# Six of sixteen pieces of the last stage's first half beside the second convolution, and a third early band of x

## The chip, the cores and the metric

One core of one Trainium2 chip runs the whole program. The metric is device time in microseconds (us). All data is float32. PE is TensorE, DVE is VectorE, ACT is ScalarE, POOL is GpSimd and SP is SyncE; an engine with a q (SPq, ACTq) is the queue of DMA issues on it.

## The reference

x has 16 samples of 128 channels and 160 x 160 pixels. For each sample:

```
x_proj = einsum('bchw,oc->bohw', x, proj_w)                # 128 -> 64 channels
att1 = route(x_proj, ..., depthwise 3x3 or 5x5)            # the kernel size is chosen by an argmax
att2 = route(att1, ..., depthwise 7x7, 9x9 or 11x11, dilation 3)
out = concatenate([att1, att2], axis=1)
maps = concatenate([out.mean(1), out.max(1)])
gate = sum over the 2 outputs of sigmoid(conv7x7(maps) + sp_b)
return out * gate + x
```

route() takes the mean over all pixels, multiplies by a small matrix and picks the convolution with the largest logit. The last stage therefore has two halves: channels 0 to 63 are att1 * gate + x (the first half, "f1"), channels 64 to 127 are att2 * gate + x (the second half, "f2").

## The kernel before

The work is a software pipeline over the samples, written as turns s = 0 to 17. In turn s the sample s is projected and gets its first convolution (att1), the sample k = s-1 gets its second convolution (att2), the sample m = s-2 gets its maps, its gate and the second half of the last stage, and the sample n = s-3 gets the first half. Turns 4 to 14 are a loop, the others are written out. Turn 16 has no new sample, turn 17 ends the last two.

PE's order in a turn sets the order of the rest. First the projection (L858, with transposes L867): x is loaded by POOL in six bands of 32 rows (load_x, L533) into two buffers, RE and RO. Bands 0 and 1 are loaded in the turn before, beside the second convolution; each later band waits until the band two before it is summed and projected. After six of thirty fills PE transposes the maps of att2 (turn_map2, L870; MAPS_AFTER = 5). ACT copies the results into X (L710). Then comes the choice (route, L898) and the 7x7 convolution (L932).

Then the first convolution (conv1, L914): 16 groups of two channel pairs, the weights prepared by ACT (L734, L740) and the result copied back to X by ACT (L745). Behind each group PE does what the table AFTER (L62) names: "gt" spreads the gate, ("f2", u) is one of five parts of the second half (nine steps of three transposes, L953, each added to x by DVE, L1274), ("f1", u) is one of sixteen pieces of the first half. A piece has 10 rows of pixels. Its life: att1 is loaded from nat_d (load_at, two buffers, 400 KB), x is loaded (load_xa, three buffers, two DMAs of 200 KB), DVE multiplies by the gate (gate1, L1288), PE transposes ten times (finish1, L963), DVE adds to x (finish1, L1298), and the sum is stored from the same buffer (store_xa). POOL issues all of that (begin1, piece1). The second half's x, 720 KB a DMA, is loaded and stored by SP, two buffers (load_xf, store_xf), and between these SP "lands" the strips of the next second convolution in L (L439).

Then the second convolution (conv2, L967): 16 groups over L, the weights loaded by ACT's queue (L761), four pairs ahead, and doubled by POOL (L591); ACT gathers the input (bring, L765) and writes the result back (L775). Beside it DVE reduces X over the channels (reduce1, L1176 and L1177), sums bands 0 and 1 of the next x (take_x, L1101), and, when 24 of 32 pairs are evacuated, reduces L to mean and maximum maps (reduce2, L1198). SP stores att1 from X to nat_d in 24 DMAs of 256-byte runs (store_att1, L449), loads the gate in G1 (L468), and copies nat_d into overlapping strips (make_strips, L463, 18 DMAs).

X holds att1 from the first convolution until store_att1 and reduce1 are through; then it is unused until the next turn's ACT writes it. Tiles of pieces lie in RA and RX, for the last three samples (late, L317) in X.

A wait in these programs stands in the stream of its engine: what follows it on that engine waits too. PE's second fill of a projection waits until all sums of the last stage so far (f1_add, f2_add) are done.

## Time and profile before

| | |
|---|---|
| median of 3 runs | 6338.1 us (6338.06 to 6348.23) |
| the profiled execution | 6353.46 us, span 6351.9 us |
| PE, DVE, ACT, POOL busy | 77%, 49%, 45%, 20% of the span |
| DMA queue q1 (SP's), q0 (POOL's), q10 (ACT's) | 39.1%, 28.2%, 8.3% of 16 engines' span |
| moved | 1285.33 MB in 1015814 packets, mean 202 GB/s |
| a steady turn, from projection to projection | 372.2 us (2802.86 to 3175.06 us) |

The profile lists the busy time of each engine; an engine's idle time costs only where the chain that ends last passes through it. "DMA share" is the mean busy share of the 16 DMA engines. In rows of the timeline the bracket at the end is the idle time of that engine just before, with what ended it. All times below are of the one profiled execution.

### The profile page before, as it was taken

The numbers are of one execution on the slowest core, as the hardware profiler recorded it, in microseconds if no ns is written. First come the engines' busy times: TensorE is split into PE (matmuls) and PEld (weight loads), VectorE is DVE, ScalarE is ACT, GpSimd is POOL, SyncE is SP. The second block draws the span as 40 slices with busy tenths as digits, with TensorE's granted clock in tenths as the row PEclk, the third lists the DMA queues.
The fourth block names the chain that finished last, engine by engine and source line by source line (L and its number), as shares of the span: only waits on it lengthen the run. The fifth ranks groups of instructions, "written<-read, shape, count | busy, mean of one in ns | idle before, by whom it ended". The sixth has DMA issues, their size and how long they took to land.

```text
span 6351.9 us, 164601 instructions
## 1 busy us (share of the span) xinstructions
PE 4896.8 (77%) x62816; PEld 3336.1 (53%) x62816; DVE 3135.5 (49%) x3835; ACT 2832.8 (45%) x5378; POOL 1256.7 (20%) x2010
## 2 busy tenths in 40 slices
PE   5678897887878788787878888787887878885453
PEld 2236464655646465564745556464555646464342
DVE  3215445464545545464554545546544554645344
ACT  3455464544545455444544545354454535452120
POOL 2001011212112121211212121121212212121332
PEclk9889898898989889798988889898798979887675
DMA  9656758869697785968779696886969688696857
GB/s 225 182 133 188 174 160 217 228 182 237 191 229 198 215 223 179 227 212 217 210 194 231 180 230 207 214 227 172 233 181 242 199 217 234 179 224 156 226 131 189
DMA packets 1015814, 1285.33 MB, mean 202 GB/s; under 512 B 670750, under 2 KB 865737, under 8 KB 984414
## 3 DMA queue, kind: packets, MB, share of 16 engines
q1 hardware_dynamic: 855500, 578.24, 39.1%
q0 software_dynamic: 90800, 555.20, 28.2%
q10 hardware_dynamic: 69026, 146.11, 8.3%
q8 instruction: 218, 3.57, 0.2%
q14 instruction: 270, 2.20, 0.1%
HBM read 950.16 MB, written 456.70 MB: 221 GB/s over the span
## 4 chain that ended last, share of the span: by engine, by line
PE 36%; DMA 33%; DVE 11%; issue 10%; ACT 3%; POOL 2%; SPq 2%; ACTq 1%; POOLq 0%; DVEq 0%
DMA out_dram<-RX 15%; PE psC L984 13%; DMA RX<-in_x_dram 8%; DVE MM L1198 7%; DMA RX<-w_d 5%; PE psA L922 5%; PE psA L923 5%; PE psA L858 5%; PE psB L953 3%; PE psB L867 2%; DMA RX<-nat_d 2%; PE psB L932 2%; PE psB L963 2%; DVE RX L1274 1%; DVE L L1255 1%
## 5 line engine op out<-in xcount | busy, mean ns | idle before, releaser
L984 PE MATMUL psC<-RX 61*60 61x96 f32 (+7 forms) x49152 | 1457.6, 266 | 231.6 <-POOL RX L591 96.2
L984 PEld LDWEIGHTS psC<-RX 61*60 61x60 f32 x49152 | 1391.2, 132 | 304.3 <-issue 300.1
L1198 DVE TENSOR_REDUCE MM<-L 124x135 f32<-124x6480 f32 (+3 forms) x128 | 527.6, 4194 | 587.4 <-ACT L L775 587.4
L775 ACT ACTIVATE L<-psC 124x120 f32 (+4 forms) x2048 | 393.8, 284 | 830.0 <-PE psC L984 791.2
L858 PE MATMUL psA<-RX,projt 128*64 128x512 f32 x1920 | 577.0, 686 | 236.2 <-DMA RX<-in_x_dram 162.2
L922 PE MATMUL psA<-X,RX 128*128 128x240 f32 x1280 | 642.1, 591 | 125.4 <-ACT RX L740 125.3
L953 PE MATMUL psB<-ident,L 124*128 124x124 f32 x2160 | 445.5, 356 | 347.5 <-DVE RX L1274 286.6
L591 POOL COPY RX<-RX 64x720 f32<-64x720 f32 x512 | 402.3, 792 | 1455.4 <-DMA RX<-w_d 1454.4
L745 ACT ACTIVATE X<-psA,bias 128x246 f32<-128x246 f32 x1024 | 638.4, 737 | 62.6 <-PE psA L923 46.2
L923 PE MATMUL psA<-X,RX 128*128 128x240 f32 x1280 | 632.5, 583 | 0.0
L734 ACT ACTIVATE RX<-RX 32x640 f32<-32x640 f32 x320 | 233.8, 735 | 880.7 <-PE psA L923 749.9
L1274 DVE TENSOR_TENSOR RX<-psB,RX 128x360 f32<-128x360 f32 (+7 forms) x1200 | 370.2, 352 | 516.5 <-DMA RX<-in_x_dram 331.1
L765 ACT ACTIVATE RX<-L 128x1080 f32 (+1 forms) x256 | 541.7, 2124 | 136.3 <-DMA L<-strip_d 136.3
L953 PEld LDWEIGHTS psB<-ident,L 124*128 124x128 f32 x2160 | 313.5, 183 | 500.1 <-issue 476.8
L1288 DVE TENSOR_TENSOR RX<-RX,G 80x1280 f32<-80x1280 f32 x208 | 307.3, 1482 | 524.7 <-DMA RX<-nat_d 506.8
L704 ACT ACTIVATE RX<-psA 128x512 f32<-128x512 f32 x480 | 287.4, 599 | 558.1 <-PE psA L858 514.4
L867 PEld LDWEIGHTS psB<-ident,RX 128*128 128x128 f32 x1920 | 215.0, 148 | 481.6 <-ACT RX L704 333.4
L1176 DVE TENSOR_REDUCE MM<-X 128x246 f32<-128x15744 f32 x16 | 264.8, 16553 | 406.8 <-ACT X L745 406.8
L922 PEld LDWEIGHTS psA<-X,RX 128*128 128x128 f32 x1280 | 292.6, 241 | 307.2 <-issue 268.8
L1101 DVE TENSOR_REDUCE part<-RX 128x1 f32<-128x4480 f32 x96 | 442.0, 4604 | 0.0
L609 POOL DMA_DIRECT2D RX<-in_x_dram x416 | 220.2, 530 | 1078.1 <-DMA out_dram<-RX 1049.6
L923 PEld LDWEIGHTS psA<-X,RX 128*128 128x128 f32 x1280 | 301.0, 235 | 210.8 <-issue 173.6
(117 smaller groups left out, 5150.9 us busy)
## 6 DMA issues: line engine op xcount, KB each, us to landing
RX<-in_x_dram POOLq DMA_DIRECT2D x64, 2560.0 KB, 11.4
RX<-w_d ACTq DMA_DIRECT2D x512, 180.0 KB, 4.4
RX<-in_x_dram SPq DMA_DIRECT2D x128, 720.0 KB, 10.6
out_dram<-RX SPq DMA_DIRECT2D x128, 720.0 KB, 14.4
nat_d<-X SPq DMA_DIRECT2D x320, 280.0 KB
RX<-nat_d POOLq DMA_DIRECT2D x208, 400.0 KB, 6.8
RX<-in_x_dram POOLq DMA_DIRECT2D x416, 200.0 KB, 5.8
out_dram<-RX POOLq DMA_DIRECT2D x416, 200.0 KB, 4.9
```

The costliest lines, as they stand in the source:

```text
L591: nc.gpsimd.tensor_copy(w2t[j][64:128, :, :], w2t[j][0:64, :, :]).then_inc(w2_doubled, 1)
L745: ins = nc.scalar.activation(X[:, :, :, c:c + 1].rearrange("p b t c -> p (b t c)"), psA[pair % 2][:, ch * N1:(ch + 1) * N1], ACT.Identity, ...
L765: nc.scalar.activation(binf[q].rearrange("p (c f n) -> p c f n", c=G, f=5), Lc[:, :, bass.ds(g * G, G)].rearrange("p (n f) c -> p c f n", ...
L775: ins = nc.scalar.activation(dst[:, 0:NU2 - par, 15 * r:15 * r + nq, par, :], src[:, par:BR:2, :, :], ACT.Identity)
L858: ins = nc.tensor.matmul(o, projt[:, :], xsb[b % 2][:, :, w0:w0 + FW], start=True, stop=True)
L922: nc.tensor.matmul(o[:, :, 0:T1], w[:, ch, 96:224], rhs, start=True, stop=False, skip_group_check=True)
L923: ins = nc.tensor.matmul(o[:, :, 1:1 + T1], w[:, ch, 224:352], rhs, start=False, stop=True, skip_group_check=True)
L953: ins = nc.tensor.transpose(psB[t % 2][:, 124 * f:124 * f + 124], L[0:124, slot * C2:slot * C2 + 128], ident[0:124, 0:124])
L984: ins = nc.tensor.matmul(o[:, :, 0:kk, a:b], w2t[2 * q + p][rows, ch, z:z + PB], src[rows, 2 * p + ch, 0:nf, 3 * cg + dc:3 * cg + dc + kk, ...
L1101: nc.vector.tensor_reduce(part[:, b, 0:1], xs[:, own, :], AX.XY, ALU.add).then_inc(x_summed, 1)
L1198: nc.vector.tensor_reduce(dst[0:124, mm, :].rearrange("p (f b k) -> p f b k", f=9, k=3)[:, :, par:BR:2, :], src[:, :, 0:NU2 - par, :, par, ...
L1274: return nc.vector.tensor_tensor(d, view(psB[t % 2][rows, :], 64 * g0 + c0, sdims), d, ALU.add)
```

## The change

The pieces 0 to 5 of the first half (EARLY = 6) of sample m are taken from the next turn's first convolution and done in this turn, beside the second convolution. SP, and not POOL, loads and stores them, from buffers in the free X (bands 1 to 3 of it). On PE the first stands behind the twelfth of sixteen groups, the next four one behind each of the last four groups, the sixth right after the fifth. The table AFTER has only the pieces 6 to 15. The third band of x gets its own buffer in X (bands 4 and 5 of it) and is loaded by SP ahead of the strips. MAPS_AFTER goes from 5 to 8. reduce2 is cut in three (32, 16 and 16 channels), its first part beginning when half the pairs are evacuated. Samples 14 and 15 keep all pieces where they were.

```diff
-MAPS_AFTER = 5
+MAPS_AFTER = 8
+EARLY = 6
+AFTER = {0: (("f1", 6),), 1: (("gt", 0), ("f1", 7)), 2: (("f2", 0),), 3: (("f2", 1), ("f1", 8)),
+         4: (("f2", 2),), 5: (("f2", 3), ("f1", 9)), 6: (("f2", 4),), 7: (("f1", 10),), 8: (("f1", 11),),
+         9: (("f1", 12),), 10: (("f1", 13),), 11: (("f1", 14),), 12: (("f1", 15),), 13: (), 14: (), 15: ()}
...
+        xbuf = [t.rearrange("p (i w) -> p i w", w=W) for t in (RE, RO, Xf[:, 10496:15616])]
+        XBUF, XNTH, XPER = (0, 1, 2, 0, 1, 0), (1, 1, 1, 2, 2, 3), (3, 2, 1)
+                self.early = self.two and self.new
...
         def _(sp):
+            sp.dma_start(xbuf[2][:, :, :], x[0, :, 2 * ROUT1 - 2:2 * ROUT1 + 30, :]).then_inc(x_loaded[2], 16)
...
+            def early_store(m, u):
+                wait_alone(sp, f1_add, 32 * m + 2 * u + 2)
+                for k in range(2):
+                    dst = ...
+                    sp.dma_start(dst, xa[1][u % 3][64 * k:64 * k + 64, :]).then_inc(early_stored[u % 3], 16)
+            def begin_early(m):
+                for u in range(2):
+                    early_load_at(m, u)
+                for u in range(3):
+                    early_load_xa(m, u)
+            def early_pieces(m):
+                for u in range(EARLY):
+                    if u + 2 < EARLY:
+                        wait_alone(sp, pr_ready, 16 * m + u + 1)
+                        early_load_at(m, u + 2)
+                    early_store(m, u)
+                    if u >= 1 and u + 2 < EARLY:
+                        q = (u + 2) % 3
+                        wait_alone(sp, early_stored[q], 32 * (among(0, EARLY, 3, q) * m + (u - 1) // 3 + 1))
+                        early_load_xa(m, u + 2)
...
                 if t.new:
+                    wait_alone(sp, att1_stored, ST1 * (s + 1))
+                    wait_alone(sp, red1_steps, s + 1)
+                    if t.early:
+                        begin_early(m)
+                    if t.next:
+                        load_x2(s + 1)
                     make_strips(s)
+                    if t.early:
+                        early_pieces(m)
...
     (POOL)
-                    wait_alone(pool, x_summed, jb - 1)
-                    wait_alone(pool, proj_mm, NF * (jb - 1))
+                    done = {3: 1, 4: 2, 5: 4}[b]
+                    wait_alone(pool, x_summed, NB1 * s + done)
+                    wait_alone(pool, proj_mm, NF * (NB1 * s + done))
...
     (ACT, in project)
                 for f in range(1, NFS):
+                    if f == NF + 1:
+                        for q in range(3):
+                            wait_alone(act, early_stored[q], 32 * among(0, EARLY, 3, q) * (s - 2))
+                    if f == 4 * NF + 1:
+                        wait_alone(act, x_summed, NB1 * s + 3)
...
     (PE)
+                    elif t.early:
+                        def groups_and_pieces(h):
+                            for q in range(2):
+                                conv2(k, 2 * h + q, q, h)
+                                finish1(m, 2 * h + q - 11, pr[1][1 - q])
+                        repeat(pe, 0, 6, groups)
+                        wait_alone(pe, f2_add, 45 * (m + 1))
+                        finish1(m, 0, pr[1][0])
+                        repeat(pe, 6, 8, groups_and_pieces)
+                        finish1(m, 5, pr[1][1])
...
     (DVE)
+                elif t.early:
+                    for mm in range(2):
+                        reduce2(k, 0, mm)
+                    wait_alone(dve, g1_loaded, 16 * (m + 1))
+                    gate1(m, 0)
+                    gate1(m, 1)
+                    for u in range(EARLY):
+                        if u in (2, 3):
+                            reduce2(k, 1, u - 2)
+                        finish1(m, u)
+                        if u + 2 < EARLY:
+                            gate1(m, u + 2)
+                    join2(k, 1)
+                    for mm in range(2):
+                        reduce2(k, 2, mm)
+                    join2(k, 2)
```

In turn 16, where sample 14's pieces lie beside the last second convolution as before, DVE does the first third of reduce2 in two parts behind pieces 9 and 11 instead of all but the last quarter behind piece 13.

## Rows read from the trace of the kernel before

**Rows 1.** The page, shares of the chain that ended last, by engine

```profile
PE 36%; DMA 33%; DVE 11%; issue 10%; ACT 3%; POOL 2%; SPq 2%; ACTq 1%; POOLq 0%; DVEq 0%
```

**Rows 2.** Stretches of turn 8: length, busy PE, PEld, DVE, ACT, POOL; clock, DMA share, GB/s

```profile
2802.86:2885.01 82.15, 63.17 (x294) 26.57 (x295) 45.92 (x82) 39.74 (x68) 11.09 (x18) 0.90 0.48 158
2885.01:2990.33 105.32, 80.28 (x317) 53.31 (x317) 58.42 (x111) 36.74 (x57) 16.62 (x30) 0.75 0.98 245
2990.33:3069.24 78.91, 68.30 (x244) 41.30 (x244) 21.73 (x28) 44.33 (x69) 23.73 (x43) 0.87 0.83 205
3069.24:3131.04 61.80, 52.96 (x1743) 50.69 (x1747) 43.62 (x11) 32.84 (x78) 15.67 (x22) 0.92 0.90 240
3131.04:3149.38 18.34, 15.93 (x572) 15.11 (x565) 0.00 (x0) 10.61 (x28) 3.91 (x5) 1.00 1.01 329
3149.38:3175.06 25.68, 21.50 (x768) 20.66 (x769) 24.93 (x5) 12.72 (x39) 5.42 (x7) 1.00 0.31 106
```

**Rows 3.** One slice of ten us, the same columns

```profile
3160.00:3170.00 10.00, 9.36 (x341) 9.05 (x343) 10.00 (x3) 4.95 (x17) 2.62 (x4) 1.00 0.09 27
```

**Rows 4.** Timeline of PE, projection of turn 8: start, us, line, tiles, idle before

```profile
2831.34 1.98 PE L858 MATMUL psA<-RX,projt 128*64 128x512 f32 x4 [8.54 <-DMA RX<-in_x_dram]
...
2850.99 1.56 PE L858 MATMUL psA<-RX,projt 128*64 128x512 f32 x4 [2.24 <-DMA RX<-in_x_dram]
...
2869.30 0.30 PE L902 MATMUL psA<-stats,projt 128*64 128x25 f32 x2
```

**Rows 5.** Timeline of POOL, the load of band 2

```profile
2821.24 0.55 POOL L548 DMA_DIRECT2D RX<-in_x_dram  x1 [3.17 <-PE psA L858]
```

**Rows 6.** Timeline of PE, pieces behind the second half

```profile
3020.30 1.04 PE L963 MATMUL psB<-ident,RX 80*128 80x80 f32 x10 [0.66 <-DVE RX L1298]
...
3030.67 1.59 PE L963 MATMUL psB<-ident,RX 80*128 80x80 f32 x10 [2.79 <-DVE RX L1298]
...
3045.39 1.60 PE L963 MATMUL psB<-ident,RX 80*128 80x80 f32 x10 [5.89 <-DVE RX L1298]
```

**Rows 7.** Stretches of turn 2, first convolution without pieces

```profile
686.11:774.68 88.57, 71.79 (x256) 45.20 (x257) 43.32 (x90) 36.92 (x57) 0.00 (x0) 0.82 0.87 204
774.68:839.87 65.19, 60.30 (x146) 28.48 (x144) 0.54 (x3) 44.11 (x69) 2.42 (x4) 1.00 0.44 90
```

**Rows 8.** Timeline of SP's queue: a reload of x, and the strips

```profile
2927.35 2.83 SPq L413 DMA_DIRECT2D RX<-in_x_dram  x2
...
3131.04 15.39 SPq L463 DMA_DIRECT2D strip_d<-nat_d  x18
```

**Rows 9.** Timeline of DVE

```profile
2946.28 0.97 DVE L1274 TENSOR_TENSOR RX<-psB,RX 128x360 f32<-128x360 f32 x2 [8.38 <-DMA RX<-in_x_dram]
...
3054.13 1.49 DVE L1288 TENSOR_TENSOR RX<-RX,G 80x1280 f32<-80x1280 f32 x1 [3.65 <-DMA RX<-nat_d]
...
3061.15 1.06 DVE L1298 TENSOR_TENSOR RX<-psB,RX 128x400 f32<-128x400 f32 x2 [4.57 <-PE psB L963]
...
3150.13 32.97 DVE L1198 TENSOR_REDUCE MM<-L 124x135 f32<-124x6480 f32 x8 [37.27 <-ACT L L775]
```

**Rows 10.** DMA issues of 2785 to 3157: KB each, median us to landing

```profile
RX<-nat_d POOLq DMA_DIRECT2D x16, 400.0 KB, 6.5
RX<-in_x_dram POOLq DMA_DIRECT2D x32, 200.0 KB, 5.9
...
RX<-in_x_dram SPq DMA_DIRECT2D x8, 720.0 KB, 10.1
```

**Rows 11.** Timeline of PE, start of the next projection

```profile
3175.06 3.08 PE L858 MATMUL psA<-RX,projt 128*64 128x512 f32 x8 [3.54 <-issue]
```

**Rows 12.** Timeline of PE, turn 16, the last piece of sample 13

```profile
5983.86 1.57 PE L963 MATMUL psB<-ident,X 80*128 80x80 f32 x10 [4.34 <-DVE X L1298]
```

**Rows 13.** Timeline of DVE, reduction of turn 16

```profile
6108.78 24.62 DVE L1198 TENSOR_REDUCE MM<-L 124x135 f32<-124x6480 f32 x4
...
6144.57 0.73 DVE L1204 TENSOR_TENSOR MM<-MM 124x243 f32<-124x243 f32 x2
```

More of the change, by code:

```diff
@@ L186, in conv_block @@
         ident_ready = sem("ident_ready")
-        x_loaded = [sem(f"x_loaded{i}") for i in range(2)]
+        x_loaded = [sem(f"x_loaded{i}") for i in range(3)]
         x_zeroed = sem("x_zeroed")
@@ L242, in conv_block @@
         pr_ready = sem("pr_ready")
+        early_at = [sem(f"early_at{i}") for i in range(2)]
+        early_xa = [sem(f"early_xa{i}") for i in range(3)]
+        early_stored = [sem(f"early_stored{i}") for i in range(3)]
         f1_mm = sem("f1_mm")
@@ L309, in wait_x, with begin_of, place, among @@
         def wait_x(eng, s, b):
-            eng.wait_ge(x_loaded[b % 2], 16 * (3 * s + b // 2 + 1))
+            eng.wait_ge(x_loaded[XBUF[b]], 16 * (XPER[XBUF[b]] * s + XNTH[b]))
         def w1_count(s, pair):
             return 16 * ((7 if pair % W1B < 2 else 6) * s + pair // W1B + 1)
-        def late(n):
-            return 1 if isinstance(n, int) and n >= B - 3 else 0
-        def xa_count(n, u):
-            return 32 * (XA[u % 3] * n + u // 3 + 1)
+        def begin_of(n):
+            return 0 if isinstance(n, int) and n >= B - 2 else EARLY
+        def place(n, u):
+            return 1 if u < EARLY or (isinstance(n, int) and n >= B - 3) else 0
+        def among(lo, hi, ring, q):
+            return sum(1 for u in range(lo, hi) if u % ring == q)
+        def before(n, ring, q):
+            full = 1 if isinstance(n, int) and n == B - 1 else 0
+            return among(EARLY, NU1, ring, q) * (n - full) + full * among(0, NU1, ring, q)
+        def is_early(n, u):
+            return u < begin_of(n)
+        def at_wait(eng, n, u):
+            q = u % 2
+            if is_early(n, u):
+                eng.wait_ge(early_at[q], 16 * (among(0, EARLY, 2, q) * n + u // 2 + 1))
+            else:
+                eng.wait_ge(at_loaded[q], 16 * (before(n, 2, q) + among(begin_of(n), u + 1, 2, q)))
+        def xa_wait(eng, n, u):
+            q = u % 3
+            if is_early(n, u):
+                eng.wait_ge(early_xa[q], 32 * (among(0, EARLY, 3, q) * n + u // 3 + 1))
+            else:
+                eng.wait_ge(xa_loaded[q], 32 * (before(n, 3, q) + among(begin_of(n), u + 1, 3, q)))
         def xf_count(m, u):
@@ L614, in store_xa @@
                     dst = bass.AP(out.tensor, n * (C * PIX) + u * (10 * W) + 5 * W * k, [[PIX, C2], [1, 800]])
-                    pool.dma_start(dst, xa[late(n)][u % 3][64 * k:64 * k + 64, :]).then_inc(out1_stored[u % 3], 16)
+                    pool.dma_start(dst, xa[place(n, u)][u % 3][64 * k:64 * k + 64, :]).then_inc(out1_stored[u % 3], 16)
             def begin1(t, n):
-                s, m = t.s, t.m
-                wait_alone(pool, f1_mm, 32 * n)
-                if late(n):
+                s, m, u0 = t.s, t.m, begin_of(n)
+                wait_alone(pool, f1_mm, 32 * n + 2 * u0)
+                if place(n, u0):
                     pool.wait_ge(att1_stored, ST1 * B)
                     pool.wait_ge(red1_steps, B)
+                    for q in range(3):
+                        pool.wait_ge(early_stored[q], 32 * among(0, EARLY, 3, q) * (B - 2))
                 else:
@@ L628, in begin1 @@
                     wait_alone(pool, min_steps, 3 * (m + 1))
-                for u in range(2):
+                for u in range(u0, u0 + 2):
                     load_at(n, u)
-                for u in range(2):
-                    wait_alone(pool, out1_stored[u], 32 * XA[u] * n)
+                for u in range(u0, u0 + 2):
+                    wait_alone(pool, out1_stored[u % 3], 32 * before(n, 3, u % 3))
                     load_xa(n, u)
@@ L645, in turn @@
                 if t.new:
-                    for b in range(2, NB1):
+                    for b in range(3, NB1):
                         if b == NB1 - 1:
@@ L653, in turn @@
                     begin1(t, n)
-                    for u in range(NU1):
+                    for u in range(begin_of(n), NU1):
                         piece1(n, u)
@@ L1317, in turn @@
                     wait_alone(dve, g1_loaded, 16 * (n + 1))
-                    for u in range(2):
+                    for u in range(begin_of(n), begin_of(n) + 2):
                         gate1(n, u)
```

128 lines of the change are left out of this document (72 added, 56 removed), and 3 rows, old and new, of the table AFTER.

## The prediction

> **What bounds the kernel now.** The page comes first: no engine is full, and the chain that ended last is split between PE, DMA and DVE [rows 1]. So I cut one steady turn out of the chain of waits (turn 8, 2802.86 to 3175.06, 372.2 us; the table of stretches splits it [rows 2]) and read each stretch by the wait that ends last in it. Thirteen turns (3 to 15) look like it; turns 0 to 2 fill the pipeline, 16 and 17 drain it.
>
> Projection and routing, 82.2 us: PE stands 8.54 us for band 2 and 2.24 us for band 5 of x [rows 4]. The load of band 2 is issued 18.4 us after PE's first projection, behind POOL's four stores of the maps and its loop [rows 5].
> First convolution until the last piece of the second half, 105.3 us: the DMA engines are full (share 0.98) [rows 2]; PE waits for x and output of the second half.
> Its rest, 78.9 us: nine groups and nine pieces of the first half. A bare group takes 7.2 us with or without a piece: turn 2 has no pieces and spends 65.2 us there [rows 7]; the 13.7 us more are waits of pieces for reloaded tiles (2.79, 5.89) [rows 6].
> Second convolution, 105.8 us with the gap behind it: PE is busy for 0.84 to 0.87, DMA for 0.90 and 1.01, then 0.31 at the end [rows 2] and 0.09 after 3160 [rows 3]. That hole is what the change fills. DVE idles 37.27 us before its reduction of 32.97 us [rows 9].
>
> **What the change adds beside the second convolution.** SP stores att1, then loads the gate, and starts the strip copies when the stores have landed, at 3131.04 [rows 8]. The early pieces need the same landing, so nothing of them starts before 3131.
> SP first issues 2 loads of att and 6 half loads of x (some 0.6 us each) and band 2 of x, 5.5 us, and then the 18 strip copies, 15.4 us, up to 3152. The data ahead of the strips is 2 x 0.41 + 3 x 0.41 + 2.62 = 4.7 MB, 14 us at the 329 GB/s of that stretch [rows 2]. The strips' transfers ended near 3161 (share 0.09 after 3160 [rows 3]) and will end near 3175.
> Pieces 0 and 1 have their tiles at about 3138 to 3144, before PE reaches them at 3149 (DVE's reduction waits for the same group and starts at 3150.13 [rows 9]): no cost but two times 0.9 us of transposes. Piece 2's att is issued at 3152, behind all strips in SP's queue. The nearest rows are the x tiles of the second half: a load issued at 2927.35 behind four landings and a store ended DVE's wait at 2946.28 [rows 8, 9], 19 us instead of the 10.1 median [rows 10]. So I let it land behind the strips, at 3176.
> The Trainium skill (DMA: Bandwidth & Descriptors, "Queues, rings and completion order") says that each DMA engine consumes the descriptors of one issuing sequencer in ring order. By that rule too the reload stands behind the strips; the 19 us agree. If it didn't hold, the first rival would be the forecast.
>
> From there the chain, with DVE in its program order: gate of 2 (1.49) to 3177.6, sum of 1 (1.06 [rows 9]), gate of 3 to 3180.1, half a reduction over 16 channels (48 of the 64 take 24.62 of 32.97 us [rows 9, 13], 16 the other 8.4, half of it 4.2) to 3184.3, sum of 2 to 3185.4. The att of 4 is issued by SP only after the store of 1, at 3182, and lands some 5 us later (3187; under load the medians are 5.9 and 6.5 [rows 10]); gate of 4 to 3188.5, the other half reduction to 3192.7, sum of 3 to 3193.8. SP meanwhile: store of 2, x of 4, att of 5 at 3189, landed at 3194.5; gate of 5 to 3196; store of 3 at 3194.4, x of 5 at 3195.8, landed at 3200.5; sum of 5 done at 3201.6. Three pieces in 19 us; the trace's nearest row, the drain of turn 16, has 1.57 + 4.34 = 5.9 us a piece [rows 12]. PE's projection cannot pass its second fill before that sum: 3202 instead of 3176.6, its start (3175.06 [rows 11]) and 1.5. **Cost +25.4 us per turn.**
> Bounds: below, the reload lands 6.5 us after its issue (3159) and only PE's transposes and one cadence are left, +9; above, each piece after 2 takes the 10.4 us that a piece took under load (3020.3 to 3030.67 [rows 6]) for 6.4, +12 more, and the strips end 5 us later, +42. I take +25.4, nearest to the drain's rows, where the DMA engines are also free.
> The Trainium skill, same page, "Anatomy of one DMA", fits 2.0 us plus bytes / 436e3 per us for a transfer, 2.9 us for a piece's 400 KB. By it three loads would each be 2 to 3 us shorter, the cost +18 and the sum 104 us lower. The trace has 6.5 and 5.9 [rows 10], so its durations stand.
> It comes in turns 2 to 15, 14 times: +356. In turn 15 PE's next work waits for DVE's reduction instead: its last quarter starts behind the sum of 5, 3201.6 and 0.7 + 8.4 + 0.7 (joins of 0.73 [rows 13]) are 3211.4 against 3183.8, +28: 3 more. In the others that is hidden: the map transposes now come after three more fills (1.6 us each), at about 3217.
> The first half of the reduction moves into DVE's idle time 3113 to 3150, free. ACT's new wait for the early stores (issued by 3204, landed by 3209) meets its sixth eviction at about 3210: nothing.
> Load of band 2 beside the weights of the second convolution: the two bands at 3075 delayed them by at most a few us; PE is early for piece 2 anyway, so nothing.
>
> **What it takes away.** Bands. Band 2 is there. Band 3 takes the place of band 2's load (20.8 us after the projection's start, since POOL still waits for the maps, and 10 us of transfer): it lands at +31, wanted at +28 (15 fills of 1.6 us, the map transposes 2.5, the start 1.4). Band 4 lands at +37, before its use at +39. Band 5 is issued when band 3 is projected, +42 with the memset before it, lands at +49 and is wanted at +47.5. Waits 3 + 1.5 for 10.8, and without the slow restarts after them (1.98 for 1.08 us a fill, some 2.5 in all): 66.4 (2802.86 to 2869.30 [rows 4]) becomes 57.5. **-9 us** (bounds 0, if POOL's issue slips with DVE, and -11). Turns 1 to 15: -135. Turn 0 gets the band too, but its 2.6 MB stand ahead of the small weights on SP: nothing, +-10.
> First convolution. Turn 2, with no piece, takes 88.6 + 65.2 = 153.8 us [rows 7] for 184.2: -30.5 is the bound for sixteen pieces. The change removes three of seven in the stretch of the second half: 15.5 x 3/7 and a little for SP's share of full DMA engines, -7; behind it six pieces for nine, of which the first three have their tiles already (the ring runs ahead while the second half is slow), leave 67 of 78.9: -12. **-19 us** (bounds -10, if the second half's loads stay as slow, and -27). Turns 3 to 15, 13 times: -247.
> Turn 16 has no convolution to hide pieces behind: three pieces less at 5.9 us [rows 12] and 8 us in the second half's stretch, -26. Its reduction, 24.62 us in front of the last pieces [rows 13], has 16 us taken out and put between pieces: -7.
> **Sum:** 356 + 3 - 135 - 247 - 26 - 7 = -56 us. The profiled execution took 6353.5 us (span 6351.9 and 1.6 around it), 15 above the median of the runs shown, 6338.1; -56 of that median is 6282. The bytes moved and all arithmetic stay the same.
>
> **Rivals.**
> 1. The reload isn't held up by the strips (+9 for +25.4 per turn): 14 x -16.4 = -230 more, 6052. For it: all sixteen engines aren't equally loaded and the strips' tail is thin. Against: the 19 us above. Between it and mine lies every earlier end of the strips. With the convolution at its bound of -27, 13 x -8 = -104, 6178 is reached as well. Together 0.25.
> 2. The other side, slower: the early pieces' chain through store, reload and DVE's order holds PE longer than the two gains. It decides from (135 + 247 + 33 - 3) / 14 = 29.4 us per turn, only 4 above my figure. At 10.4 us a piece and late strips, +42 per turn, +232: 6514; at +34, 6402. For it: DVE does gate 2 before sum 1, so one late tile holds both, and PE is idle in between and restarts slower. Against: the DMA engines are nearly idle then. 0.30.
> 3. The first convolution stays bound by the second half's tiles and gives 10: 13 x 9 = +117, 6399, slower too. For it: share 0.98 with the landings, which stay. Against: turn 2. 0.08.
> 4. Nothing: what is gained in one stretch is given back in the other within 0.2%. 0.07.
> My forecast 0.30 in its own range of 6230 to 6325.
>
> **How the numbers follow.** A change under 0.2% (13 us) can't be told from none. Faster: the forecast (nearly whole) and rival 1, and 0.02 of what lies just outside 0.2% in rival 4: 0.57. Same: 0.08 (rival 4 and the edge of the forecast's). Slower: rivals 2 and 3 without their own edges: 0.35. The terms' bounds (+-8 x 14, +-6 x 13, +-2 x 15) give about +-130; the range 6140 to 6440 leaves out the ends of rivals 1 and 2.
>
> **What would show it.** Right: PE idle 10 to 16 us between the last quarter's second and third group, ended by DVE's gate, itself by the att tile; first projection near 128 us after the second convolution's start (103.3 before); waits for bands under 5 us; first convolution 163 to 168 us; DMA share 0.6 or more in the old hole. Wrong: a third piece before 3165 in the turn's time (rival 1), or pieces 3 to 5 more than 8 us apart (rival 2), or the stretch of the second half still over 100 us (rival 3).

## The result, and the profile after

The changed kernel takes 6244.6 us (median of 4 runs, 6239.9 to 6256.7) against 6343.2 us (6338.1 to 6348.2) for the kernel before: a ratio of 0.985 with the interval 0.983 to 0.987. It is 1.5% faster, 99 us where 56 were forecast. Measured again with the first experiments it came to 0.987 (0.984 to 0.989). The profiled execution took 6248.6 us, span 6246.9 us. It lies near the median of its kernel, while the profiled one of the kernel before lies 10 us above: differences between the two traces come out some 6 us larger than those between medians (-104.9 us for -98.5).

The page of the kernel after, busy times and the shares of the chain that ended last, by engine [rows 1] and by line:

```profile
PE 4902.2 (78%) x62816; PEld 3305.9 (53%) x62816; DVE 3144.4 (50%) x3931; ACT 2831.7 (45%) x5378; POOL 1030.5 (16%) x1574
...
PE 34%; DMA 23%; SPq 21%; issue 9%; DVE 8%; ACT 2%; ACTq 1%; POOL 1%; DVEq 0%; POOLq 0%
SPq L485 12%; PE psA L1011 9%; PE psA L1012 9%; DMA X<-nat_d 6%; DMA out_dram<-RX 6%; DMA RX<-in_x_dram 5%; PE psC L1074 4%; SPq L535 4%; PE psA L947 3%; PE psB L1042 3%; SPq L436 3%; PE psB L1021 2%; PE psB L1053 2%; DVE MM L1299 2%; PE psB L956 2%
```

PE, DVE and ACT are as busy as before within a point, POOL is less busy (16% for 20%). SP's queue, 2% of the old chain, has 21% of the new one: 12 of these are the stores of att1 (L485), for which the early pieces wait, and 4 the strips (L535). The pieces now hang on what SP issues and in which order.

Stretches of turn 8 of the kernel after (2776.55 to 3145.27, 368.7 us for 372.2): projection and routing, second half, rest of the first convolution, and the second convolution in four parts, split where SP loads the early pieces, where it reloads the third, and in the last groups. Columns as in [rows 2]:

```profile
2776.55:2846.43 69.88, 60.46 (x294) 25.68 (x295) 45.57 (x82) 39.71 (x68) 10.57 (x17) 0.94 0.49 154
2846.43:2944.38 97.95, 77.31 (x297) 51.91 (x298) 52.99 (x102) 36.72 (x57) 10.89 (x20) 0.76 0.98 236
2944.38:3012.62 68.24, 63.72 (x206) 33.58 (x205) 15.03 (x20) 46.77 (x70) 15.13 (x27) 1.00 0.72 170
3012.62:3070.49 57.87, 50.26 (x1635) 48.26 (x1639) 42.33 (x12) 28.83 (x73) 12.77 (x17) 0.91 0.94 251
3070.49:3098.00 27.51, 23.08 (x688) 22.12 (x683) 18.45 (x7) 12.06 (x32) 5.47 (x7) 0.88 1.02 290
3098.00:3125.00 27.00, 15.69 (x408) 14.22 (x412) 4.61 (x7) 9.75 (x23) 5.21 (x6) 0.81 0.75 256
3125.00:3145.27 20.27, 15.11 (x414) 14.31 (x414) 14.69 (x14) 3.08 (x16) 0.62 (x1) 0.84 0.69 181
```

Most signs named ahead for a right forecast are there: first convolution 166.2 us (163 to 168), stretch of the second half under 100, waits for bands under 5 us, DMA share over 0.6 in the old hole; the next projection starts 132.7 us after the second convolution's first matmul (forecast near 128, before 103.3). One is not: PE's wait for DVE in the last quarter is 5.99 us and not 10 to 16. The first three lines are the gain: 69.88 for 82.15 us, 97.95 for 105.32, 68.24 for 81.46. The other four are the price: 132.7 us for 103.3. (The table [rows 2] divides 2.55 us earlier, where ACT's gather begins, hence its 78.91 and 105.8.) The hole at the end of the second convolution, DMA share 0.31 before, is filled (0.75 and 0.69). But PE is busy there for only 15.69 of 27.00 us, and its granted clock, 1.00 before, is 0.81.

What PE waits for there, the timeline of PE (start, length, line, idle before):

```profile
3106.91 1.49 PE L1053 MATMUL psB<-ident,X 80*128 80x80 f32 x10
...
3123.10 1.59 PE L1053 MATMUL psB<-ident,X 80*128 80x80 f32 x10 [5.99 <-DVE X L1406]
3124.86 7.19 PE L1074 MATMUL psC<-RX 61*60 61x135 f32 x192 [0.17 <-issue]
...
3132.82 5.41 PE L1074 MATMUL psC<-RX 61*60 61x135 f32 x192
...
3140.09 1.04 PE L1053 MATMUL psB<-ident,X 80*128 80x80 f32 x10 [1.02 <-DVE X L1406]
3145.27 3.68 PE L947 MATMUL psA<-RX,projt 128*64 128x512 f32 x8 [4.14 <-issue]
```

In this kernel L1053 are the transposes of pieces (L963 before), L1074 the second convolution. PE stands 5.99 us before the third piece, for a sum on DVE. The timeline of DVE says what that sum waited for:

```profile
3085.68 2.88 DVE L1397 TENSOR_TENSOR X<-X,G 80x1280 f32<-80x1280 f32 x2
3097.62 1.06 DVE L1406 TENSOR_TENSOR X<-psB,X 128x400 f32<-128x400 f32 x2 [9.06 <-PE psB L1053]
3121.07 1.49 DVE L1397 TENSOR_TENSOR X<-X,G 80x1280 f32<-80x1280 f32 x1 [22.39 <-DMA X<-nat_d]
...
3131.53 1.49 DVE L1397 TENSOR_TENSOR X<-X,G 80x1280 f32<-80x1280 f32 x1 [1.41 <-DMA X<-nat_d]
...
3144.68 1.06 DVE L1406 TENSOR_TENSOR X<-psB,X 128x400 f32<-128x400 f32 x2 [4.17 <-DMA X<-in_x_dram]
```

The gate of piece 2 (L1397) waits 22.39 us for att1, and the sum of piece 1 (L1406), which PE needs, stands behind it in DVE's program. SP's queue and then the chain of waits of the same stretch close the circle:

```profile
3070.49 0.83 SPq L492 DMA_DIRECT2D X<-nat_d  x2
3071.50 3.92 SPq L499 DMA_DIRECT2D X<-in_x_dram  x6
3075.62 0.43 SPq L489 DMA_DIRECT2D X<-in_x_dram  x1
3076.40 21.23 SPq L535 DMA_DIRECT2D strip_d<-nat_d  x18
3098.00 0.34 SPq L492 DMA_DIRECT2D X<-nat_d  x1
```

```profile
3064.81 5.39 DMA nat_d<-X
...
3098.00 22.94 DMA X<-nat_d
...
3127.04 4.35 DMA X<-nat_d
```

The reload for piece 2 (L492, the second row of that line in SP's list) is issued behind all 18 strip copies, at 3098.00, and lands 22.94 us later. The next reload on the chain, piece 4's at 3127.04, takes 4.35 us.

The projection of the same turn, on PE, SP and DVE:

```profile
2821.58 1.08 PE L947 MATMUL psA<-RX,projt 128*64 128x512 f32 x4 [1.56 <-DMA RX<-in_x_dram]
...
2831.42 0.27 PE L991 MATMUL psA<-stats,projt 128*64 128x25 f32 x2 [1.03 <-DVE stats L1205]
```

```profile
2797.41 17.49 SPq L436 DMA_DIRECT2D map_d<-RX  x12
```

```profile
2824.50 0.82 DVE L1332 TENSOR_TENSOR minc<-RX,minc 48x640 f32<-48x640 f32 x1 [9.65 <-DMA minc<-map_d]
```

Of the waits for bands, 8.54 and 2.24 us before [rows 4], 1.56 is left. DVE now stands 9.65 us for the maps, for which it did not wait before; they come later (MAPS_AFTER = 8), and its last sums of x stand behind that wait: PE's first matmul of the routing (L991, L902 before) waits 1.03 us for them, and in other turns more.

### The profile page after: what moved, and what is told of

Same layout as the page of the kernel before. It is cut to its first block, busy times and chain, and to the rows that moved or that the text cites. A ratio compares the mean times of both kernels' runs of the same rounds, so it can differ in the third digit from the quotient of the medians.

```text
span 6246.9 us, 164652 instructions
## 1 busy us (share of the span) xinstructions
PE 4902.2 (78%) x62816; PEld 3305.9 (53%) x62816; DVE 3144.4 (50%) x3931; ACT 2831.7 (45%) x5378; POOL 1030.5 (16%) x1574
## 4 chain that ended last, share of the span: by engine, by line
PE 34%; DMA 23%; SPq 21%; issue 9%; DVE 8%; ACT 2%; ACTq 1%; POOL 1%; DVEq 0%; POOLq 0%
SPq L485 12%; PE psA L1011 9%; PE psA L1012 9%; DMA X<-nat_d 6%; DMA out_dram<-RX 6%; DMA RX<-in_x_dram 5%; PE psC L1074 4%; SPq L535 4%; PE psA L947 3%; PE psB L1042 3%; SPq L436 3%; PE psB L1021 2%; PE psB L1053 2%; DVE MM L1299 2%; PE psB L956 2%
## 5 line engine op out<-in xcount | busy, mean ns | idle before, releaser
L1074 PE MATMUL psC<-RX 61*60 61x120 f32 (+7 forms) x49152 | 1538.6, 273 | 327.9 <-issue 154.7
L1074 PEld LDWEIGHTS psC<-RX 61*60 61x60 f32 x49152 | 1462.0, 137 | 404.4 <-issue 398.3
L671 POOL COPY RX<-RX 64x720 f32<-64x720 f32 x512 | 416.4, 816 | 1828.5 <-DMA RX<-w_d 1825.2
L1042 PE MATMUL psB<-ident,L 124*128 124x124 f32 x2160 | 413.4, 334 | 323.8 <-DVE RX L1383 283.2
L834 ACT ACTIVATE X<-psA,bias 128x246 f32<-128x246 f32 x1024 | 636.9, 735 | 56.6 <-issue 30.5
L1299 DVE TENSOR_REDUCE MM<-L 124x135 f32<-124x2160 f32 (+1 forms) x192 | 535.3, 2843 | 243.9 <-ACT L L864 243.9
L947 PE MATMUL psA<-RX,projt 128*64 128x512 f32 x1600 | 462.9, 662 | 138.5 <-DMA RX<-in_x_dram 50.1
L1042 PEld LDWEIGHTS psB<-ident,L 124*128 124x128 f32 x2160 | 290.6, 172 | 471.3 <-issue 445.9
L1011 PEld LDWEIGHTS psA<-X,RX 128*128 128x128 f32 x1280 | 267.0, 219 | 338.3 <-issue 314.8
L1397 DVE TENSOR_TENSOR X<-X,G 80x1280 f32<-80x1280 f32 x126 | 190.5, 1522 | 444.1 <-DMA X<-nat_d 434.9
L1012 PEld LDWEIGHTS psA<-X,RX 128*128 128x128 f32 x1280 | 284.0, 222 | 231.1 <-issue 212.7
L1011 PE MATMUL psA<-X,MM 128*128 128x240 f32 x768 | 383.7, 588 | 16.5 <-ACT MM L829 14.9
L1012 PE MATMUL psA<-X,MM 128*128 128x240 f32 x768 | 379.5, 583 | 0.0
## 6 DMA issues: line engine op xcount, KB each, us to landing
L<-strip_d SPq DMA_DIRECT2D x192, 405.0 KB, 12.4
```

The costliest lines, as they stand in the source:

```text
L671: nc.gpsimd.tensor_copy(w2t[j][64:128, :, :], w2t[j][0:64, :, :]).then_inc(w2_doubled, 1)
L834: ins = nc.scalar.activation(X[:, :, :, c:c + 1].rearrange("p b t c -> p (b t c)"), psA[pair % 2][:, ch * N1:(ch + 1) * N1], ACT.Identity, ...
L947: ins = nc.tensor.matmul(o, projt[:, :], xsb[b][:, :, w0:w0 + FW], start=True, stop=True)
L1011: nc.tensor.matmul(o[:, :, 0:T1], w[:, ch, 96:224], rhs, start=True, stop=False, skip_group_check=True)
L1012: ins = nc.tensor.matmul(o[:, :, 1:1 + T1], w[:, ch, 224:352], rhs, start=False, stop=True, skip_group_check=True)
L1042: ins = nc.tensor.transpose(psB[t % 2][:, 124 * f:124 * f + 124], L[0:124, slot * C2:slot * C2 + 128], ident[0:124, 0:124])
```

## The experiments

Each was timed beside the kernel before on the same chip. The table has the mean over turns 4 to 14 of each one's profiled execution, in us, from the start of one stage's first matmul to that of the next. "Projection" ends at the last projection matmul. "Second half" ends with its last transposes. "C2, 3/4" and "C2, 1/4" are the second convolution's first three quarters and the last, "next" the time from its last matmul to the next projection, which holds the sixth piece where there is one (5.2 us between the convolutions are the same in all). after_again is another execution of the changed kernel: its columns differ from the first one's by up to 1.4 us. e8 changes nothing in the projection and yet has 61.5 us there for 64.2. So a difference of 1 to 3 us in one column shows nothing by itself; the ratios are from all executions.

| kernel | ratio (interval) | projection | routing | second half | rest | C2, 3/4 | C2, 1/4 | next | turn |
|---|---|---|---|---|---|---|---|---|---|
| before | 1 | 64.2 | 17.6 | 104.0 | 77.4 | 79.1 | 22.3 | 3.7 | 373.4 |
| after | 0.985 (0.983-0.987) | 53.4 | 19.7 | 95.5 | 63.5 | 83.1 | 41.3 | 7.1 | 369.0 |
| after_again | 0.987 (0.984-0.989) | 53.7 | 18.9 | 96.8 | 63.5 | 82.2 | 42.7 | 7.1 | 370.2 |
| e1_band_only | 0.975 (0.972-0.977) | 51.8 | 17.6 | 101.6 | 75.9 | 80.5 | 23.3 | 3.7 | 359.7 |
| e2_pieces_only | 0.995 (0.993-0.998) | 64.5 | 17.6 | 96.5 | 63.3 | 79.5 | 37.2 | 7.1 | 370.7 |
| e4_band_late | 0.969 (0.966-0.973) | 52.5 | 19.6 | 96.2 | 63.5 | 80.2 | 36.4 | 7.4 | 361.1 |
| e3_late_maps5 | 0.968 (0.964-0.972) | 54.2 | 17.6 | 95.9 | 63.5 | 79.7 | 37.1 | 6.9 | 360.2 |
| e5_reload_first | 0.964 (0.960-0.968) | 53.2 | 20.0 | 96.5 | 63.6 | 78.9 | 31.2 | 10.7 | 359.4 |
| e6_all_tiles | 0.962 (0.957-0.967) | 52.0 | 17.9 | 95.6 | 63.4 | 80.8 | 36.4 | 6.2 | 357.5 |
| e7_no_strips | 0.951 (0.947-0.955) | 52.0 | 19.1 | 95.8 | 63.4 | 82.2 | 28.3 | 6.2 | 352.2 |
| e8_split_loop | 0.999 (0.997-1.000) | 61.5 | 17.6 | 103.2 | 76.7 | 78.5 | 23.7 | 3.9 | 370.3 |
| e9_strips_last | 0.977 (0.975-0.979) | 56.7 | 25.7 | 96.3 | 63.5 | 80.4 | 31.9 | 6.2 | 366.0 |
| e10_last_maps5 | 0.978 (0.976-0.980) | 56.6 | 25.7 | 95.7 | 63.7 | 81.2 | 31.1 | 6.2 | 365.4 |

**Each half of the change alone.** e1_band_only keeps the third band beside the second convolution and leaves all sixteen pieces where they were:

```diff
-EARLY = 6
+EARLY = 0
-MAPS_AFTER = 8
+MAPS_AFTER = 5
...
-                self.early = self.two and self.new
+                self.early = False
...
 (AFTER as in the kernel before)
```

> The third band of x alone, all sixteen pieces in the first convolution, map transposes after six fills as before (the reduction stays cut in three). Theory (the parts are separate terms, and beside the second convolution they collide): projection 64 -> 53 us in turns 1 to 15, nothing lost elsewhere, 15 x -10 = -150, 6180 to 6205 us. Rival (the kernel is bound by the bytes of a turn, which don't change): the wait for bands comes back as a wait for other transfers, at most -50, 6290 or more.

6166.7 us (6149.8 to 6181.0). The band alone gives 2.5%, more than the whole change, and slightly more than expected. In the table it is worth 12.4 us in the projection and 3.9 in the first convolution, for 2.4 in the second. The 3.9 were not expected, but e8, which leaves that stage as it was, has 1.5 of them too.

e2_pieces_only moves the pieces and loads no third band:

```diff
-        xbuf = [t.rearrange(...) for t in (RE, RO, Xf[:, 10496:15616])]
+        xbuf = [t.rearrange(...) for t in (RE, RO)]
...
-                    if t.next:
-                        load_x2(s + 1)
...
```

> The six pieces alone, all bands of x as before. Theory (piece 2's att stands in SP's queue behind the strips and behind whatever is ahead of them, the band's 2.6 MB too): without the band the tile lands 8 us earlier, the second convolution costs +18 per turn instead of +26, the first gives -22, and with turns 16 and 17 the kernel takes 6255 to 6285 us. Rival (the 23 us of the tile are due to the strips alone, or the end of the stretch is set by the weights): +26 per turn stay, less the bands' -9 the kernel takes 6340 to 6380 us.

6303.4 us (6299.0 to 6311.9): 0.5% faster than before, between the two expectations. The second convolution's stage costs 18.7 us more and the first convolution gives 21.6. So the pieces are nearly break-even by themselves. Alone the halves give 13.7 and 2.7 us a turn; together 4.4, so they cost each other 12: 5.3 in the second convolution, 3.4 in projection and routing, 3.1 in the first convolution (where e1's 3.9 doesn't come on top). The 12 are too large, since the table's execution of the kernel before is among its slowest, and those of e1 and e2 are their fastest. By the medians on one chip the halves give 165.9 and 29.3 us in the whole program and together 78.9 (after_again): they cost each other 116 us, 8 to 9 a turn.

**The band behind the pieces.** e4_band_late moves one DMA of 2.6 MB from ahead of the strips to behind the pieces:

```diff
-                    if t.next:
+                    if t.next and not t.early:
                         load_x2(s + 1)
                     make_strips(s)
                     if t.early:
                         early_pieces(m)
+                        if t.next:
+                            load_x2(s + 1)
```

> The changed kernel, the load of the third band moved on SP from in front of the strips to behind the last early piece (turns 2 to 14). It is wanted some 20 us after the projection starts and takes 10. Theory: piece 2's tile lands 8 us earlier, PE's projection starts 7 to 8 us earlier, no wait for the band: 12 x -8 = -95, 6135 to 6165 us. Rival (another wait, the weights' transfers or DVE's order, ends at the same time): the tile lands earlier but the projection moves by under 3 us, 6210 or more.

6136.1 us (6121.7 to 6166.2), as expected: 7.9 us a turn from one line's place, 7.8 of them in the second convolution. They come in two parts of the path of piece 2's tile (means over turns 4 to 14). SP needs 14.9 us for issuing the strips and not 19.4, and the reload behind them lands after 18.9 us and not 22.3. DVE of turn 8, at the gate of piece 2:

```profile
3070.15 1.49 DVE L1399 TENSOR_TENSOR X<-X,G 80x1280 f32<-80x1280 f32 x1 [17.54 <-DMA X<-nat_d]
```

It waits 17.54 us for 22.39. And the band needs no earlier place: the projection is no slower (52.5 for 53.4).

e3_late_maps5 is e4_band_late with MAPS_AFTER = 5:

> The kernel with the band loaded late (0.969 of before), and the map transposes after six fills of the projection again, not nine. In the changed kernel the reduction ended at 3155.48 and the transposes came at 3162.24, and the maps' way through SP then held up the 7x7 convolution: the time from last projection to first convolution was 17.6 us in some turns and 20 to 23 in others. Theory: that stretch is 17.6 in every turn, -2 us per turn, 6105 to 6125 us. Rival (PE waits for the reduction instead, in front of fills that hide nothing): the projection grows by 1 to 3 us, no gain, 6130 to 6165.

6132.7 us (6120.1 to 6140.9). The routing is back at 17.6 us, the projection is 1.7 longer: 0.9 us a turn, within the runs' scatter. The rival's result; the mechanism of the theory is seen in the rows and is worth next to nothing.

**What the reload waits for.** e5_reload_first, beside the late band, issues the reloads of att1 for pieces 2 and 3 after twelve of the eighteen strip copies:

```diff
-                        make_strips(s)
+                        make_strips(s, (0, 1))
+                        reload_at(m, 0)
+                        reload_at(m, 1)
+                        make_strips(s, (2,))
                         early_pieces(m)
```

> The band late, and on SP the reloads of att for pieces 2 and 3 issued behind two thirds of the strip copies instead of all of them. Theory (SP's queue is served in order): piece 2's tile lands 6 to 8 us earlier still, the end of the second convolution moves by 3 to 6 us, 6060 to 6110 us. Rival (the queue's order doesn't matter, transfers share the engines): the tile lands when it did and the time stays at 6125 to 6165.

6110.4 us (6090.3 to 6116.8), as expected or a hair above. SP and DVE of it:

```profile
3042.04 0.99 SPq L492 DMA_DIRECT2D X<-nat_d  x2
3043.21 6.08 SPq L540 DMA_DIRECT2D strip_d<-nat_d  x6
```

```profile
3058.00 1.49 DVE L1409 TENSOR_TENSOR X<-X,G 80x1280 f32<-80x1280 f32 x1 [15.14 <-DMA X<-nat_d]
3059.41 1.04 DVE L1418 TENSOR_TENSOR X<-psB,X 128x400 f32<-128x400 f32 x2
3060.37 1.48 DVE L1409 TENSOR_TENSOR X<-X,G 80x1280 f32<-80x1280 f32 x1
...
3074.07 1.49 DVE L1409 TENSOR_TENSOR X<-X,G 80x1280 f32<-80x1280 f32 x1 [7.09 <-DMA X<-nat_d]
```

Issued at 3042.04 behind twelve strip copies it still lands only at 3058, 16 us later (15.5 in the mean). The last quarter is 5.2 us shorter than in e4; 3.3 come back in the gap behind it, since piece 4 now has the late tile (7.09 us).

e7_no_strips is the changed kernel without the strip copies from turn 2 on, and without the wait for them, so the second convolution reads old strips; that part of the computation is left out:

```diff
-                    make_strips(s)
+                    if not t.early:
+                        make_strips(s)
...
```

> The changed kernel with the strip copies left out from turn 2 on (this part of the computation is missing: the second convolution reads old strips). Theory (piece 2's tile waits behind the strips): it lands some 6 to 8 us after its issue instead of 23, PE doesn't wait for it, the last quarter takes 26 to 31 us instead of 41, -11 to -14 per turn; with nothing else changed 6060 to 6110 us. Rival (store, reload and DVE's order are the cost): under -5 per turn, 6180 or more.

6025.5 us (6008.3 to 6036.6), below the expected range. DVE at its gates of pieces 2 and 3:

```profile
2998.47 1.48 DVE L1397 TENSOR_TENSOR X<-X,G 80x1280 f32<-80x1280 f32 x1
...
3005.30 1.49 DVE L1397 TENSOR_TENSOR X<-X,G 80x1280 f32<-80x1280 f32 x1 [0.58 <-DMA X<-nat_d]
```

Piece 2 waits for nothing, with the 2.6 MB of the band ahead of it as in the changed kernel; its reload, issued at 2987.69, has landed before 2998.47. So of the 19.0 us that the last quarter lost, 13.0 go with the strips (41.3 to 28.3) and 6.0 stay with the pieces. It shows that the strips are the larger part of the cost. It does not show that the reload's wait is all of the 13.0, since the strips' transfers and their time in SP's queue are gone for everything else too; e6 takes the waits away alone.

**Tiles for all pieces.** If the chain of buffers is the cost, it goes with six own tiles each for att1 and x, all loaded ahead of the strips. e6_all_tiles does that, band late:

```diff
+        eat = [Xf[0:PX1, o:o + 1280]... for o in (0, 1280, 10496, 11776, 13056, 14336)]
+        exa = [Xf[:, 5184 + 800 * u:5984 + 800 * u] for u in range(6)]
...
-                for u in range(3):
-                    early_load_xa(m, u)
+                for u in range(EARLY):
+                    early_load_xa(m, u)
+                    if u + 2 < EARLY:
+                        early_load_at(m, u + 2)
```

> The band late, and all six early pieces with tiles of their own for att and x in the free X, all loaded ahead of the strips, so that no piece waits for a reload or a store. Theory (the reloads are the cost of the pieces): PE passes the last quarter of the second convolution at its own pace plus six pieces and some wait for weights, 22.3 -> 28 to 31 us for 36.4, the gap behind it 4 to 7 us, together -8 to -12 us per turn, 5995 to 6050 us. Rival (the weights' transfers behind the strips hold PE, or DVE's order does): the tiles are early and the stretch still takes over 34 us, 6100 or more.

6095.3 us (6066.6 to 6113.5). The theory missed: the last quarter is 36.4 us, as long as e4's. PE and SP of it:

```profile
3024.32 0.91 PE L1053 MATMUL psB<-ident,X 80*128 80x80 f32 x10
...
3034.42 2.77 PE L1074 MATMUL psC<-RX 61*60 61x80 f32 x53 [4.63 <-issue]
...
3048.59 0.57 PE L1074 MATMUL psC<-RX 61*60 61x80 f32 x5 [3.90 <-issue]
3049.09 1.60 PE L1053 MATMUL psB<-ident,X 80*128 80x80 f32 x10
3050.62 7.37 PE L1074 MATMUL psC<-RX 61*60 61x135 f32 x192
```

```profile
3014.31 21.46 SPq L533 DMA_DIRECT2D strip_d<-nat_d  x18
```

No wait for a tile is left. What replaced it are gaps inside two groups of matmuls, 4.63 and 3.90 us, which no semaphore explains, and the lower clock behind them (7.37 us for a group of 192 that takes 5.41 at full clock). The same gaps, smaller, stand in the changed kernel (2.32, 1.90 and 0.88 us). e6 is still the fastest complete version of all, 3.8% under the kernel before. Of its 3.6 us a turn against e4 only 0.6 are in the second convolution and the gap behind it; 2.2 are in projection and routing, no more than single executions differ by.

The trace does say what PE waits for in the gaps. The DMA view of the first one, from 3029.8 to 3034.4, has one transfer of 16 KB on the queue that carries the program's code:

```profile
q8 instruction: 1, 0.02, 1.5%
```

Its packet starts at 3031.93 and lands at 3033.00, and PE goes on 1.42 us later. The one in the second gap lands at 3047.36, 1.23 us before PE goes on. It is so everywhere. The traces of before, after, e1, e2 and e4 to e9 have 403 gaps of over 0.8 us between two matmuls of the second convolution in which no semaphore is waited for; 401 of them end 1.2 to 1.7 us behind the landing of a 16 KB transfer on q8, where a moment picked at random does so in some 2% of cases. So these are waits for code. In the last quarter they make up 5.7 us a turn in the changed kernel, 3.1 in e4, 7.3 in e6, 4.5 in e9, 1.6 without the strips (e7) and none over 0.8 us in the kernel before (means over turns 4 to 14). That is why e6 missed: it took away the waits for tiles, and waits for code grew in their place. The share of the DMA engines between the gaps is 1.01 (3030 to 3050); that the full engines hold the code up is argued from this and from e7, not shown apart.

One guess on record was that PE's loop, now cut in two (groups 0 to 11, then 12 to 15), makes it fetch new code at a bad moment. e8_split_loop cuts the loop of the kernel before and changes nothing else:

```diff
-                    else:
+                    elif t.two:
+                        repeat(pe, 0, 6, groups)
+                        repeat(pe, 6, 8, groups)
+                    else:
                         repeat(pe, 0, 8, groups, t.first)
```

> The kernel before, with one edit: PE's loop over the second convolution is written as two loops of the same body, 6 and 2 iterations, in turns 2 to 15, as the changed kernel has it, but without pieces. Theory (PE stands inside groups 12 to 14 for the instructions of the second loop, which come by DMA, 16 KB at a time, and are late while the strips fill the engines): 5 to 9 us more per turn in the last quarter of the second convolution, 6390 to 6450 us. Rival (those gaps belong to the pieces' waits): no change, 6320 to 6345.

6325.5 us (6306.8 to 6339.3), 0.999 (0.997 to 1.000): the cut costs nothing that can be told from noise, and the 5 to 9 us a turn of the theory are not there. Its trace does have more waits for code than the kernel before: 4.8 us a turn for 1.9, 4.2 of them in the first three quarters, though the second convolution with the gap is only 1.0 us longer. So the cut alone doesn't bring waits of the size of the changed kernel's into the last quarter; it has 0.6 us a turn there.

e9_strips_last has e6's tiles, and all pieces, their stores and the band issued ahead of the strips:

```diff
-                    if t.next:
-                        load_x2(s + 1)
-                    make_strips(s)
                     if t.early:
                         early_pieces(m)
+                    if t.next:
+                        load_x2(s + 1)
+                    make_strips(s)
```

> All six early pieces with tiles of their own, and the strip copies issued on SP behind the stores of the pieces and the third band, not ahead. Theory (the strips' transfers in the last third of the second convolution hold up weights and instructions): the last quarter takes 27 to 30 us as without strips, for 36.4, the bands lose 0 to 3 us to the strips, 5970 to 6040 us. Rival (the gaps stay, or the strips take as much from the projection and the maps as they gave): 6070 to 6110 us as with the strips ahead.

6190.3 us (6185.9 to 6212.3), slower than e6 by 1.5 points and outside both expectations. SP's queue:

```profile
3089.95 36.33 SPq L508 DMA_DIRECT2D out_dram<-X  x12
3126.51 0.41 SPq L492 DMA_DIRECT2D X<-in_x_dram  x1
3127.61 15.50 SPq L533 DMA_DIRECT2D strip_d<-nat_d  x18
...
3151.21 29.41 SPq L439 DMA_DIRECT2D map_d<-RX  x12
```

Last quarter and gap together are 38.1 us, for 42.6 in e6 and 41.9 in e5. But the strips now meet the next projection's bands (projection 56.7 us for 52.0), and the copies of the maps (L439) take 29.41 us behind them for 17.49 in the changed kernel, so the routing waits (25.7 for 17.9). Its PE still has a wait for code, 3.83 us. The engines were full then, with the strips not yet issued (the stores of the pieces and other loads were): the DMA share of that slice, second number from the end, is 1.04. The transfer lands at 3095.52, 1.39 us before PE goes on:

```profile
3096.91 2.77 PE L1072 MATMUL psC<-RX 61*60 61x80 f32 x53 [3.83 <-issue]
...
3101.14 7.38 PE L1072 MATMUL psC<-RX 61*60 61x135 f32 x192
...
3109.30 5.40 PE L1072 MATMUL psC<-RX 61*60 61x135 f32 x192
```

```profile
3093.00:3097.00 4.00, 0.17 (x5) 0.09 (x8) 0.00 (x0) 0.54 (x4) 0.00 (x0) 0.76 1.04 241
```

e10_last_maps5 asked whether earlier maps (MAPS_AFTER = 5) undo that:

> The same with the map transposes after six fills. Theory: SP issues the maps' copies behind the strips, so they are late by SP's 15 us of issue; transposes three fills earlier gain 0 to 3 us per turn over the version with nine, 5950 to 6030 us. Rival (SP is still busy with the strips when the maps are ready, so their time is set by SP): no difference, within 10 us.

6201.9 us (6189.7 to 6217.8), 0.978 for e9's 0.977: no difference that can be told from noise, near what the rival said. The maps' copies are late because of the strips and not because of when they are made.

## Why the prediction was right, step by step

The sign and the mechanism of the cost were right; the size was 49 us short in the spans (-104.9 for -56) and 43 by the medians (-98.5). By turns, in us (the measured ones from the starts of the projections in both traces; turn 15 ends with the first transpose of the maps in turn 16, behind the reduction):

| turns | forecast | measured |
|---|---|---|
| start, 0 and 1 | -9 | -14.7 |
| 2 | +16 | +9.2 |
| 3 to 14 | -31 | -49.7 |
| 15 | 0 | -11.4 |
| 16 and 17 | -33 | -38.3 |

**The cost beside the second convolution: right.** Forecast +25.4 a turn, measured +26.4 (4.0 + 19.0 + 3.4). Step by step in turn 8: piece 2's reload is issued behind the strips and lands 22.94 us later (forecast 24, from [rows 8, 9]), DVE's gate holds the sum of piece 1, and from that gate to the end of piece 5's sum are 24.7 us (3121.07 to 3145.74; forecast 25.6, from 3176 to 3201.6). e7 shows the strips as the cause. One term was too small: SP needed 21.23 us for issuing the strips (19.4 in the mean) where 15.4 were taken over from before. With it turn 8 alone cost 29.4 us (132.7 for 103.3); that the mean over the turns is so near the forecast is in part luck. PE's wait for DVE in the last quarter was forecast as one of 10 to 16 us and is 5.99: some of that time it lost earlier, to waits for code inside groups (2.32, 1.90 and 0.88 us before 3117), a term that the forecast did not have, and to its clock. And e6 shows that the time is not won by removing the waits for tiles alone.

The rule of the Trainium skill (DMA: Bandwidth & Descriptors, "Queues, rings and completion order") that a DMA engine takes one sequencer's descriptors in ring order agrees with the reload at 3098.00; e5 agrees too, with 16 us behind twelve copies. No run here separates the order in the ring from the share of the engines that the strips take. The fit of the Trainium skill (same page, "Anatomy of one DMA"), which it states for DMAs that gpsimd issues, gives, as an estimate, 2.9 us for 400 KB; SP's reload for piece 4 in turn 8 took 4.35 us, and the median of that turn's six was 6.4. The measured durations gave the right sum.

**"Load of band 2 beside the weights ... so nothing": wrong.** This is the step that failed. Its 2.6 MB were counted into the landing of the strips, but the step took them as given and asked only whether the weights suffer. e4 puts the same load behind the pieces: 2.9 us less in the first three quarters and 4.9 in the last. The load ahead costs the reload 4.5 us of SP's issuing and 3.4 us of landing, as measured above. So the change gave 1.5% where its own parts, otherwise ordered, give 3.1%. The cost stood inside the +25.4, which is why the sum did not suffer; a reader who wanted a better kernel would have been led past it.

**Bands: right as a sum.** Forecast -9, measured -10.8 in the projection and +2.1 in the routing, -8.7. "Hidden" was wrong for the later maps: DVE's wait of 9.65 us for them passes to the routing in some turns. With MAPS_AFTER = 5 (e3) the routing is 17.6 in the mean and the projection 1.7 slower. Turn 0, forecast nothing, gave 11.0.

**First convolution: direction right, size small.** Forecast -19 (-7 and -12), measured -22.4 (-8.5 and -13.9). The rest of it, 63.5 us, is down to turn 2's bare stretch [rows 7], forecast 67: the pieces left there cost nothing more. e2 has the same gain without the band. These 3.4 us a turn, less 1.0 that the cost was larger, and a turn 3 that gave only 0.8, make most of the 19 us that turns 3 to 14 gave beyond the forecast. Of the 49 in all, 11 are in turn 15, 7 in turn 2, 6 before it and 5 in turns 16 and 17.

**Edges.** Turn 15, forecast 0 with +28 for the reduction, gave -11.4: there is no next sample, so neither bands 0 and 1 nor band 2 stand beside the second convolution, the tiles land earlier, and its last quarter is 5.1 us longer instead of 19. PE's wait for the reduction behind it is 18.45 us for 13.78 before. Turns 16 and 17 gave 5 us more than forecast (their reduction, cut, gives 8.1 for 7).

**The rivals.** Rival 1 (the reload isn't held by the strips) is refuted by the 22.94 us and e7. Rival 2's break-even for the whole change was 29.4 us a turn, for 26.4 measured. The pieces by themselves pay little: 21.6 us a turn gained for 18.7 in e2, 0.5% in all. In the presence of the band as the change places it, the pieces do harm: 0.985 with them (0.987 on e1's chip), 0.975 without (e1). Rival 3 falls with the first convolution's 22.4, rival 4 with the 1.5%.

**Still open.** What delays the code in the waits inside PE's groups: that they are waits for code is shown, that the strips and stores ahead of it in the DMA engines make them long is argued. In the gap of 4.63 us in e6 the transfer's packet starts only 2.14 us after PE has stopped. No version changes only the place of the code. Whether the band alone shortens the first convolution by more than single executions differ is open too.

## What to carry to other kernels

When work moves beside other work, list what its own loads stand behind in the queue that issues them, and try the order before anything else: the place of one 2.6 MB load was worth more than the whole change (7.9 us a turn for 4.4). Measure the parts of a change alone, since here one part gave more than both. A small load that someone waits for goes ahead of bulk copies, but the bulk isn't free at the back either: moved to the end it met the next stage (e9). An idle time without a semaphore inside a run of equal matmuls can be a wait for code: look in the DMA view whether the instruction queue moved something just then. And a chain of waits that is cut shows only what it hid: e6 won 0.6 us in the second convolution where 8 to 12 were expected.

## What the runs showed of the hardware

A 400 KB load issued behind the 18 strip copies took 22.94 us to land in turn 8, and piece 4's load 4.35; the median of the six of the turn is 6.4. With two thirds of the copies ahead (e5) it was still 16. Copies ahead slow the issue itself too. The eighteen strip copies took 14.9 us of SP's queue in e4 and 19.4 with a load of 2.6 MB ahead (after). The twelve of the maps took 17.49 us, and 29.41 right behind the strips (e9).

PE went on 1.2 to 1.7 us after a 16 KB transfer of the instruction queue had landed, in 401 of the 403 gaps of over 0.8 us in the second convolution that no semaphore explains; the longest of these gaps was 5.53 us (e9).

Idle time on PE costs twice here. After the stand of 5.99 us the granted clock is near its lower level (0.5 in the profile's figure, 1.2 of 2.4 GHz), and the next group of 192 matmuls takes 7.19 us, where the one after it takes 5.41. Two slices of ten us of the kernel after, columns as above:

```profile
3110.00:3120.00 10.00, 4.33 (x136) 3.67 (x132) 0.00 (x0) 3.40 (x10) 1.45 (x3) 0.92 0.74 251
3120.00:3130.00 10.00, 6.74 (x140) 6.52 (x142) 8.93 (x8) 1.10 (x4) 2.14 (x2) 0.57 0.53 135
```

PE idles for more than half of the first slice, and the clock of the second is 0.57.
